# Attention with key scores between projections, query weights on turned heads, outs by threes; retention's end reordered

## The reference

```python
# 1. attention over x, 16 heads of 32
q = (ln(x) * qn_w + qn_b) @ q_w + q_b;  k, v = split((ln(x) * kvn_w + kvn_b) @ kv_w + kv_b)
q, k = rotary(q), rotary(k)        # with a radius from x @ rh_w, which scales them
q, k = (ln(a) * ln_w + ln_b for a in (q, k))     # over the 32 of a head
x = ln(x + softmax(q @ k.T / sqrt(32)) @ v @ out_w + out_b)
# 2. retention: queries from x, keys and values from ctx
q, k, v = xpos(x @ Wq), xpos_inverse(ctx @ Wk), ctx @ Wv
x = ln(x + (q @ k.T * decay_mask(0.96875)) @ v)
# 3. coupling, three times, then a last ln
t = sigmoid(gelu(gelu(gelu(y @ w1 + b1) @ w2 + b2) @ w3 + b3) @ w4 + b4)
y = y + (0.1 + range * (0.7 * gate(mean(x)) + 0.3 * t - 0.5) * 2) * twist(y)
```

## Time and profile before

| | us |
|---|---|
| median of 3 runs | 2050.43 |
| lowest, highest | 2050.31, 2058.86 |
| the profiled execution | 2052.32 |
| its span, first to last instruction | 2050.4 |
| attention's start, to 131 | 131 |
| attention's loop, to 1089.2 | 958.2 |
| retention, 1099 to 1559 | 460 |
| coupling | 491.4 |

### The profile page before, as it was taken

The page is one execution under the profiler, slowest core; times in us unless marked ns, Lnnn a source line. Parts: engine busy times, 40 slices in busy tenths (PEclk is TensorE's granted clock), DMA queues, the critical chain, the costliest instruction groups (busy, mean ns, idle before and its releaser), DMA issues. The chain is left out here.

```text
span 2050.4 us, 26478 instructions
## 1 busy us (share of the span) xinstructions
PE 1777.7 (87%) x8648; PEld 1329.2 (65%) x8648; DVE 1455.5 (71%) x2915; ACT 1258.5 (61%) x2674; POOL 861.0 (42%) x802
## 2 busy tenths in 40 slices
PE   6788888888888888888888999999986999999972
PEld 5556566666566665666536878787775777777751
DVE  7768677686776867767655767676653678888876
ACT  3388777886868868688693232322323667777764
POOL 3677678676876768768521222222220000000000
PEclk9799999999999999999889999999997999999996
DMA  4222232322323223222252101111121011111111
GB/s 151 58 77 62 57 98 62 94 61 62 93 62 98 57 61 94 62 78 57 69 168 108 62 36 48 54 55 57 62 88 41 21 42 62 62 62 62 42 41 62
DMA packets 86184, 141.06 MB, mean 69 GB/s; under 512 B 16544, under 2 KB 19616, under 8 KB 86048
## 3 DMA queue, kind: packets, MB, share of 16 engines
q1 hardware_dynamic: 86048, 139.37, 22.0%
HBM read 63.82 MB, written 25.17 MB: 43 GB/s over the span
## 5 line engine op out<-in xcount | busy, mean ns | idle before, releaser
L526 DVE TENSOR_REDUCE a_neg_max<-a_max 128x1 fp32r<-128x512 f32 x512 | 340.4, 684 | 175.4 <-PE a_max L911 173.3
L796 ACT ACTIVATE a_probs<-a_exp 128x512 f32<-128x512 f32 x512 | 294.2, 606 | 209.6 <-PE a_exp L929 208.7
L775 ACT ACTIVATE a_max<-a_max,a_neg_max 128x512 f32<-128x512 f32 x512 | 347.1, 689 | 15.3 <-DVE a_neg_max L526 13.5
L911 PE MATMUL a_max<-a_stack 96*128 96x512 f32 x512 | 224.7, 463 | 92.3 <-ACT a_max L775 84.6
L368 POOL TENSOR_TENSOR a_rstd<-a_rstd,a_minus_half 128x16 f32<-128x16 f32 x64 | 186.0, 2906 | 90.4 <-DVE a_rstd L510 90.3
L911 PEld LDWEIGHTS a_max<-a_stack 96*128 96x128 f32 x512 | 99.1, 197 | 190.7 <-ACT a_max L775 141.0
L886 PE MATMUL a_t<-a_w_hi,a_zT_hi 128*128 128x384 f32 x500 | 181.5, 363 | 32.8 <-DVE a_v L491 23.0
L1717 POOL TENSOR_TENSOR f_yrstd<-f_yrstd,f_minus_half 128x4 f32<-128x4 f32 x8 | 11.0, 1376 | 472.0 <-DVE f_yrstd L1736 472.0
L929 PE MATMUL a_exp<-a_stack 100*128 100x512 f32 x512 | 192.0, 416 | 9.9 <-ACT a_probs L796 6.5
L887 PE MATMUL a_t<-a_w_lo,a_zT_hi 128*128 128x384 f32 x500 | 173.4, 347 | 0.0
L888 PE MATMUL a_t<-a_w_hi,a_zT_lo 128*128 128x384 f32 x500 | 173.2, 346 | 0.0
(11 more groups left out here) (286 smaller groups left out, 4919.7 us busy)
## 6 DMA issues: line engine op xcount, KB each, us to landing
a_stack<-a_nT_hi SPq DMA_DIRECT2D x512, 64.0 KB, 2.0
a_stack<-a_nT_lo SPq DMA_DIRECT2D x256, 64.0 KB, 2.0
a_z<-x SPq DMA_DIRECT2D x8, 1024.0 KB, 7.9
a_y<-x SPq DMA_DIRECT2D x8, 1024.0 KB, 5.7
r_xn<-x SPq DMA_DIRECT2D x8, 1024.0 KB, 5.6
r_cn<-ctx SPq DMA_DIRECT2D x8, 1024.0 KB, 7.9
x<-r_xn SPq DMA_DIRECT2D x16, 512.0 KB, 2.8
f_xn<-x SPq DMA_DIRECT2D x8, 1024.0 KB, 5.6
```

The costliest lines, as they stand in the source:

```text
L526: nc.vector.tensor_reduce(neg_max[:, t, ROW + h:ROW + h + 1].bitcast(F32R), bank_max[i % NB][:, :], AX_X, ALU.max, negate=True).then_inc(m ...
L775: nc.scalar.activation(bank_max[i % NB][:, :], bank_max[i % NB][:, :], ACT.Exp, bias=neg_max[:, t, ROW + h:ROW + h + 1], accum_out=sums[:, ...
L796: nc.scalar.activation(probs[:, kt % 2, h, :], bank_exp[i % 2][:, :], ACT.Exp).then_inc(exp_done, 1)
L911: mm(bank_max[i % NB][:, :], stack[0:ROW, par, h, t * P:(t + 1) * P], stack[0:ROW, par, HG + h, :], start=True, stop=True).then_inc(score_ ...
```

## The change

In attention:
- `KS_DONE` moves key scores ahead, and from slot 1 on key scores and projection items alternate, a key score first. In slot 0 the order stays. `WEIGH_AT` moves the first three weighings ahead.
- ScalarE takes the first square, and the high part of the last unit's output, before the slot's exponentials.
- The query's head weights leave GpSimd (two operations of 128x512). They are applied after the turn, when the head's 32 values lie on partitions: one `tensor_scalar` on VectorE in place in PSUM, `weight_heads`, between TensorE's turn and ScalarE's high part, with two new semaphores. The weights are loaded by eight small transfers in place of two.
- GpSimd adds the output bias between `centre` and `head_norm`, not at the unit's end.
- The statistics of x are two steps in slots of their own; its final moments (`x_final`) and root move from unit g = 3 into the next g = 0, slot 3, its shift to slot 7, its normalisation to slots 8 to 11.
- `out_item` is now one group of three products, sixteen in slots 2 to 10.

In retention:
- `x_stats` goes ahead of rotation 2, `x_norm` is halved, its first half ahead of rotation 3; `v_out` 0 goes ahead of `kq_out` 2. `norm` is named as `moments` and `out`, which in the steady list stand side by side.
- In the last batch four splits are left, behind the last scores; the other five run on ScalarE and VectorE in the coupling phase after the first turns. w1 is loaded first, with a semaphore of its own. The last stores are waited for in the coupling phase, where their rows or their tile are used.

```diff
-KS_DONE = tuple(min(4 * (i + 1) // 3, T * HG) for i in range(16))
+KS_DONE = (2, 5, 7, 8, 9, 10, 11, 12, 13, 14, 15, 16, 16, 16, 16, 16)
-WEIGH_AT = (5, 7, 10, 13)
+WEIGH_AT = (3, 5, 9, 13)
-OUT_AT, ADD_AFTER = (4, 5, 7, 9), (4, 6, 8, 10)
+OUT_DONE, ADD_AFTER = (0, 0, 1, 3, 4, 6, 8, 10, 12, 14, 16, 16, 16, 16, 16, 16), (4, 6, 8, 10)
-X_NORM_AT, STATS_AFTER, FINAL_AFTER, SHIFT_AFTER = (6, 7, 8, 9), (5, 7), 9, 4
-VAR_AFTER, SQUARE_AT = (2, 3), (1, 2)
+X_NORM_AT, STATS_AFTER, FINAL_AFTER, SHIFT_AFTER = (8, 9, 10, 11), (5, 8, 9, 11), 3, 7
+VAR_AFTER, SQUARE_AT = (1, 2), (0, 1)
...
-        loads += [(head_w[:, :], w["ln_w"].partition_broadcast(P)), (head_b[:, :], w["ln_b"].partition_broadcast(P))]
+        loads += [(head_wb[h * HD:(h + 1) * HD, i:i + 1], w[name].rearrange("(n o) -> n o", o=1))
+                  for h in range(HG) for i, name in enumerate(("ln_w", "ln_b"))]
...
-                if c == 0:
-                    last.then_inc(pool_step, 1)
-                    pool.wait_ge(pool_step, steps.next())
-                    hw, hb = (a[:, :].unsqueeze(1).broadcast_to((P, T * HG, HD)) for a in (head_w, head_b))
-                    nc.gpsimd.tensor_tensor(n[:, c], n[:, c], hw, ALU.mult).then_inc(pool_step, 1)
-                    pool.wait_ge(pool_step, steps.next())
-                    last = nc.gpsimd.tensor_tensor(n[:, c], n[:, c], hb, ALU.add)
...
+            def weight_heads(U, bank):
+
+                dve.wait_ge(nT_done, 2 * U + 2)
+                if not counts(U):
+                    dve.wait_ge(weights_done, 1)
+                nc.vector.tensor_scalar(bank[:, :], bank[:, :], head_wb[:, 0:1], head_wb[:, 1:2], ALU.mult, ALU.add).then_inc(weighted, 1)
...
+                    if left >= 2 and i == SQUARE_AT[0]:
+                        square(U + 2, 0)
+                    if i == ATTN_HIGH_AT and counts(U):
+                        attn_hi(U - 1, (g - 1) % G)
                     for m in within(KS_DONE, i):
                         exps(U, m)
-                    if i == ATTN_HIGH_AT and counts(U):
-                        attn_hi(U - 1, (g - 1) % G)
...
-                    if left >= 3:
-                        for m in within(PROJECT_DONE, i):
+                    items = list(within(PROJECT_DONE, i)) if left >= 3 else []
+                    keys = list(within(KS_DONE, i))
+                    for n_item in range(max(len(items), len(keys))):
+                        if i == 0:
+                            break
+                        if n_item < len(keys):
+                            key_scores(U, g % 2, keys[n_item])
+                        if n_item < len(items):
+                            project_item(b, g, items[n_item])
+                    if i == 0:
+                        for m in items:
                             project_item(b, g, m)
-                    for m in within(KS_DONE, i):
-                        key_scores(U, g % 2, m)
+                        for m in keys:
+                            key_scores(U, g % 2, m)
...
-    ("pair", "now", 2), ("kq_out", "now", 1), ("rotate", "now", 2), ("pair", "now", 3),
-    ("rotate", "now", 3), ("x_stats", "next", 0), ("v", "now", 0), ("kq_out", "now", 2), ("x_norm", "next", 0), ("v", "now", 1),
-    ("v_out", "now", 0), ("v_out", "now", 1), ("turn", "next", (0, 0)), ("turn", "next", (0, 1)),
+    ("pair", "now", 2), ("kq_out", "now", 1), ("x_stats", "next", 0), ("rotate", "now", 2), ("pair", "now", 3),
+    ("x_norm", "next", 0), ("rotate", "now", 3), ("v", "now", 0), ("v_out", "now", 0), ("kq_out", "now", 2),
+    ("v", "now", 1), ("v_out", "now", 1), ("x_norm", "next", 1), ("turn", "next", (0, 0)), ("turn", "next", (0, 1)),
...
-    ("mask", 2), ("c_split", 0), ("s_out", 1), ("c_split", 1), ("scores", 3), ("s_out", 2),
-    ("c_split", 2), ("mask", 3), ("c_split", 3), ("weigh", 0), ("s_out", 3), ("weigh", 1),
-    ("add", 0), ("c_split", 4), ("add", 1), ("norm", 0), ("weigh", 2), ("c_split", 5), ("weigh", 3),
-    ("add", 2), ("c_split", 6), ("c_split", 7), ("c_split", 8), ("add", 3), ("norm", 1)]
+    ("mask", 2), ("s_out", 1), ("scores", 3), ("s_out", 2), ("mask", 3), ("weigh", 0), ("s_out", 3), ("weigh", 1),
+    ("add", 0), ("add", 1), ("moments", 0), ("c_split", 0), ("weigh", 2), ("add", 2), ("out", 0), ("weigh", 3),
+    ("add", 3), ("moments", 1), ("c_split", 1), ("c_split", 2), ("c_split", 3), ("out", 1)]
...
-                act.wait_ge(cou.load, 16 * 4)
+                act.wait_ge(cou.load_first, 16)
...
+            if "split" in do:
+                for i in range(K, 9):
+                    do["split"](i)
```

More of the change, by code:

```diff
@@ L388, in unit @@
                         centre(U + 2, s)
+                if g >= 2:
+                    for t in range(2 * (g - 2), 2 * (g - 1)):
+                        add_bias(b, t)
+                if left >= 2:
                     for s in range(2):
                         head_norm(U + 2, s)
-                if g == 3 and more:
-                    x_rstd(b + 2)
+                if g == 0 and b >= 1 and b + 1 < B:
+                    x_rstd(b + 1)
                 if left >= 3:
@@ L608, in unit @@
                             head_var(U + 2, s, g == 2)
+                    if left >= 2 and i == TURN_AT[g > 0][1]:
+                        weight_heads(U + 2, bank_t[1])
                     for s in range(2):
@@ L612, in unit @@
                     if g >= 2 and more and i in STATS_AFTER:
-                        x_stats(b + 2, 2 * (g - 2) + STATS_AFTER.index(i))
-                    if g == 3 and more and i == FINAL_AFTER:
-                        x_final(b + 2)
+                        t, half = divmod(STATS_AFTER.index(i), 2)
+                        (x_stats if half else x_variance)(b + 2, 2 * (g - 2) + t)
+                    if g == 0 and 1 <= b < B - 1 and i == FINAL_AFTER:
+                        x_final(b + 1)
                     if g == 0 and left == 4 and i == SHIFT_AFTER:
@@ L729, in _ @@
             spread_max(0, 0)
-            for s in range(2):
-                turn_low(1, s, bank_t[s])
+            turn_low(1, 0, bank_t[0])
+            weight_heads(1, bank_t[1])
+            turn_low(1, 1, bank_t[1])
             run(unit)
@@ L1050, in unit @@
                             z_item(b, t)
-                    for t in range(T):
-                        if g == 0 and counts(b) and i == OUT_AT[t]:
-                            out_item(b, t)
+                    if g == 0 and counts(b):
+                        for m in within(OUT_DONE, i):
+                            out_item(b, m)
             for t in range(T):
@@ L1177, in splits @@
                 (self.w4.broadcast_to((P, P)), 1.0, self.w4_hi[:, :], self.w4_lo[:, :])]
+        out += [(self.raw1[:, k, :], -1.0, self.w1_hi[:, K + k - 1, :], self.w1_lo[:, K + k - 1, :]) for k in (1, 2)]
         return out
@@ L1324, in out_rstd @@
                 nc.gpsimd.tensor_tensor(yshift[:, par, at], yshift[:, par, at], yrstd[:, par, at], ALU.mult).then_inc(yshift_done, 1)
[L1326 removed]
+            run({"x_stats": x_rstd, "rotate": rotate, "moments": out_rstd})
             pool.wait_ge(cou.load_small, 16 * 7)
@@ L1345, in x_stats, with normalise_x @@
                 nc.vector.tensor_scalar(rstd[:, :], moments[:, :, 1], 1.0, EPS, ALU.mult, ALU.add).then_inc(xvar_done, 1)
-            def normalise_x(b, par, _):
+            def normalise_x(b, par, half):
                 dve.wait_ge(xrstd_done, b + 1)
-                for t in range(T):
+                for t in (2 * half, 2 * half + 1):
                     nc.vector.tensor_scalar(xn[:, par, t, :], xn[:, par, t, :], moments[:, t, 0:1], rstd[:, t:t + 1],
@@ L1756, in first_low, with split @@
                 lower(h1_lo[:, par, j, :], full1[:, j % 2, :], h1_hi[:, par, j, :]).then_inc(first_lo, 1)
+            def split(i):
+                raw, sign, hi, lo = cou.splits()[i]
+                dve.wait_ge(cou.split_high, i + 1)
+                nc.vector.scalar_tensor_tensor(lo, raw, sign, hi.bitcast(F32), ALU.mult, ALU.subtract).then_inc(cou.split_low, 1)
             def gate(b, par, step):
@@ L1894, in turned, with split @@
                                      ACT.Copy).then_inc(t_hi, 1)
+            def split(i):
+                raw, sign, hi, lo = cou.splits()[i]
+                act.wait_ge(cou.load, 16 * 3)
+                nc.scalar.activation(hi, raw, ACT.Copy, scale=sign).then_inc(cou.split_high, 1)
             def gelu(full, hi, bank, bias):
@@ L1903, in first_out @@
                 act.wait_ge(first_done, K * b + j + 1)
+                if b == 0 and j == 0:
+                    act.wait_ge(cou.split_low, 7)
                 if counts(K * b + j - 1):
@@ L2023, in second @@
             def second(b, par, j):
+                if b == 0 and j == 0:
+                    pe.wait_ge(cou.split_low, 9)
                 pe.wait_ge(first_saved, K * b + min(j + 2, K))
```

95 lines of the change are left out of this document (47 added, 48 removed).

## The result

The changed kernel takes 2037.7 us (median of 7, 2034.1 to 2041.5); the kernel before, beside it, 2052.8 (2050.3 to 2058.9). The ratio is 0.993, 95% interval 0.9915 to 0.9945: faster by 0.7%. Forecast were 1991 us, range 1955 to 2030. The direction was right, the size wrong by 47 us. The profiled execution took 2037.7 us and spans 2035.5.

The account below looks back on a forecast made before the run. TensorE, busy 87% of the span, leaves only its idle time to win; in attention three engines hold each other up. Terms -15 - 1.4 - 13 + 1.4 - 31 = -59 took 2050.4 to 1991 us, range 1955 to 2030.

Parts of the forecast that it names:

- Key scores and outs: Attention units: interleaved key scores and outs by threes feed ScalarE and cut TensorE's idle time; -31 us, bounds -89 to +39.
- The new wait: Third key score of each attention unit: TensorE idles some 1.4 us for ScalarE's exponential, now behind the high part.
- Query weights: Attention: GpSimd loses two operations per unit, VectorE gains one of 0.70 us, hidden; 0, uncovered +22 us.
- Biases and x statistics: Attention: moved bias additions, spread statistics and later final moments, which no one waits for; 0, between -5 and +5 us.
- Start: Kernel's start: weight operation and two hand-overs come before the query's low split that gates stack transfers; +1.4 us, bounds 0 and +2.
- Retention's x: Retention's batches: the 2.2 us wait for x goes, 1.1 us of idle stays; -15 us in seven batches, bounds 0 and -20.
- Last batch and seam: Retention's last batch, longest v wait removed, -1.4 us; its end, hole closed and store no longer waited for, -13 us.
- Moved splits: Coupling phase's start: five moved weight splits fit beside the first pass in ScalarE's and VectorE's idle time; 0, uncovered 3 us.
- attention gives nothing back: Rival for attention: new 1.4 us wait equals the interleaving's saving, or VectorE becomes the bound; 2022 us, chance 0.20.
- The slower rival: Third key score of each unit: TensorE's stand also brings a 1.2 GHz stretch, +36 us in all; 2058 us, chance 0.06.

Follow-up runs that it names:

- e4: Changed kernel with old slots of key scores and weighings, projections ahead of key scores, exponentials ahead of the high part on ScalarE: 2000.2 us, ratio 0.973.
- i2: Changed kernel with only the old KS_DONE and WEIGH_AT tables restored; alternation and ScalarE's order stay: 2001.5 us, ratio 0.9754.
- f2: Kernel of e4 with the query head weights again as two operations on GpSimd: 2000.3 us, ratio 0.9747.
- e2: Changed kernel with bank 0's low part ahead of the new weight operation on VectorE in units g 1 to 3: 2040.0 us, ratio 0.992.
- g3: Kernel of e4 with bank 0's low part ahead of the weight operation on VectorE: 2000.2 us, ratio 0.9748.
- h3: Kernel of e4 with outs again by twelves and query weights again on GpSimd, both together: 2013.9 us, ratio 0.9801.

## Why the prediction was right or wrong, step by step

*Key scores and outs, -31 predicted: the step that failed.* The key scores cost 41 us (e4 against the change) and the outs alone gave nothing measurable. The new wait itself was right in kind: 1.4 us forecast, 33.7 us in 28 units measured, 1.2 each and up to 1.7. Three things in the step were wrong.

I set it against TensorE's idle time, as if 1.1 us of old waits would be left. The waits in g 1 to 3 came to 3.5 to 3.9 us a unit (3.2 to 3.5 before), under other names, where I had 2.5. "Everything on TensorE is queued behind it" stood in the text, but I did not ask which of it the unit was waiting for: the first query score, 2.2 us late.

I took TensorE's bank waits for the measure of what could be won. The Trainium skill (Perfetto Trace Analysis, Optimization Strategies) says that in general the matmul engine should be kept as busy as possible and the engines that block the critical path be sped up. The trace agrees as far as the whole goes: TensorE's idle time from 131 us to attention's end is 122 us after the change and 115 in i2. It doesn't hold of one kind of wait: a unit of g 1 to 3 has the length of its onset plus 21 to 24 us of query scores that go round TensorE, VectorE and ScalarE through three banks, and the kernel with 46.0 us of bank waits beats the one with 28.7 by 36 us. Nor did the clock by itself set a unit's length, though it accounts for some of the time: beside the unit of 28.70 us at granted clock 1.00 above, the same unit a batch earlier is as long at 0.88:

```profile
412.20:440.90 28.70, 25.22 (x124) 17.39 (x125) 23.25 (x47) 24.06 (x56) 22.07 (x20) 0.88 0.22 54
```

TensorE's busy time there is 1.57 us more and its idle time as much less. It isn't always free: in g 1 the changed kernel has 28.37 us at 1.00 and 29.11 and 29.16 at 0.94 and 0.90.

I took the engine that starves most, ScalarE, for the one to feed. It was fed with the work that nobody waited for (key exponentials), ahead of the work on which the unit's end hangs.

*Query weights, 0:* right as far as one edit shows (f2), though the operation took 0.81 us where 0.70 was taken, and TensorE got a wait of 20.4 us from it that e2 and g3 show to be off the path. That it saves g 0 when the outs come by twelves (h3) was not seen.

*Biases and x statistics, 0 within 5:* too small. They give 11 us in the kernel of e4. I had said that nobody waits for either; with the old places the row maxima of g 2 stand behind two statistics in one slot of VectorE. *Squares and variances* had no price of their own; they give 12 us. For the squares the traces show the gain in the onsets, for the statistics in the rest of g 2 and the onset of g 0. Some of it is the clock: in the six middle batches TensorE is at 1.2 GHz for 44.4 us with the old statistics and for 23.9 in e4. By which wait each of them gains was not taken apart.

*Start, +1.4:* the first query scores began at 67.63 and not 68.16, so -0.5; GpSimd's two operations had been ahead of the turn, which I had not set against the added ones.

*Retention's x, -15:* the mechanism right, the size half. The wait for x is gone and the granted clock is 1.00 through all steady batches, but the v waits are 2.2 us a batch where I left 1.1 (waits of TensorE, 1104 to 1543 us, against the earlier trace rows):

```profile
PE r_t L1497 <- DVE r_v_lo L1398: 15.4, 14, 1.6
```

The statistics of four tiles follow each other in 53.57 us per batch where they took 54.35 and 54.95 by turns: 1.08 a batch, -7.6 in seven. The prediction had put rotation 3's end 1 us behind the transposes; v's low part, queued behind it and behind two normalisations of 1 us each, ends at 1197.66, 1.61 us after TensorE wants it.

*Last batch and seam, -14.4:* 21.8 less 7.6 is 14.2. Both the closed hole and the store no longer waited for show as forecast (0.9 us against "about 1"). *Moved splits, 0:* the coupling phase is 1.1 us longer here, but over the executions profiled, with the same coupling code, it lasts 492.5 to 495.7 us against 491.4 here before, so the price is 1 us or a few and no closer.

*The sum:* 5.8 us later for attention in place of 29.6 earlier (-31 and the start's +1.4) is 35 of the 44 us between forecast and span; retention's batches are 7, the coupling phase 1. *Rivals:* nearest was the first, "attention gives nothing back", 2022, but the gain was not nothing: 30 us given and 41 taken. That attention came out near its "nothing back" is the balance of two terms that it did not have. The slower rival named the right place, the third key score, with the wrong price (a stretch at 1.2 GHz); its 1.2 us were read between a unit of g 1 and one of g 2, while within g 1 of the kernel before 0.94 against 1.00 is 0.8 to 1.0 us (28.05 to 28.23 against 27.21). The forecast had said it would be wrong if units g 1 to 3 stay at 28 us: they did.

What stays open: through which waits the squares, the statistics and the outs with the weights give their 30 us and how much of it is the clock (in batches 1 to 6 of the kernel before one unit of g 2 and none of g 3 is at 1.00 throughout, so there is hardly anything to compare at equal clock); why the early slots cost 13 us (7 by the raw medians) even with the projections first; and whether alternating from slot 2 on costs anything.

## What to carry to other kernels

Where engines pass work round in a ring, find the chain whose start fixes the stage's end and measure its onset: an edit that puts even short work ahead of that chain's first item can cost its length plus every stand inside it (here 0.7 and 1.58 us, for an onset 1.9 to 2.2 us later), however much idle time it fills elsewhere. Bank waits that fall prove nothing: a wait of TensorE of 20.4 us in all could here be cut to 6.5, and in another kernel one of 16.8 removed, without a gain. An edit that seems hidden should be priced by whether it comes before the onset, and undone alone and in pairs, since one of two edits may be enough. And where the granted clock differs between two kernels, compare units at the same clock before you give the difference to an edit.

## What the runs showed of the hardware

The copy of the inverses on VectorE (128x512, SBUF to SBUF) takes 0.43 us or, mostly, 1.05 to 1.26, in the same kernel. Kernel before, two of them, and GpSimd beside the long one:

```profile
453.24 1.12 DVE L543 COPY a_inverses<-a_sums 128x512 f32<-128x512 f32 x1
490.13 0.43 DVE L543 COPY a_inverses<-a_sums 128x512 f32<-128x512 f32 x1
...
453.03 1.05 POOL L370 TENSOR_TENSOR a_n<-a_n,a_rstd 128x512 f32<-128x512 f32 x1
```

The long one starts 0.2 us after a GpSimd multiplication and ends 0.28 us after it. The Trainium skill (SBUF — State Buffer, Who interferes with whom) says that a VectorE operation in a two-port mode and one of GpSimd exclude each other, the later one waiting until the other is done; the trace agrees for this pair. The mean of this copy fell from 0.88 to 0.73 us with the change, 5 us of VectorE's time in 32 copies.

The weight operation, in place in PSUM with two operands per partition, takes 0.81 to 0.82 us in all 32, where the two-tensor operations in PSUM take 0.68 to 0.70.
